# A start-up stretch on VectorE put in another order: the low parts of the first pair of batches

## The reference

```
q = rms_norm(layernorm(x) @ Wq)              # 32 heads of 128
k = rms_norm([context, layernorm(x)] @ Wk)   # 8 key heads, 256 keys per batch
v = [context, layernorm(x)] @ Wv
x = x + tanh(g) * (softmax(q k' / sqrt(128)) v) @ Wo
```

## Time and profile before

| | us |
|---|---|
| median of 3 runs | 1226.1 |
| lowest and highest | 1225.43, 1226.37 |
| the profiled execution | 1224.71 |
| its span in the trace | 1223.0 |
| TensorE busy | 1169.9 (96%) |
| VectorE busy | 832.4 (68%) |
| ScalarE busy | 588.2 (48%) |
| GpSimd busy | 348.8 (29%) |

### The profile page before, as it was taken

The page is one execution under the profiler, slowest core; times in us unless marked ns, Lnnn a source line. Parts: engine busy times, 40 slices in busy tenths (PEclk is TensorE's granted clock), DMA queues, the critical chain, the costliest instruction groups (busy, mean ns, idle before and its releaser), DMA issues.

```text
span 1223.0 us, 20618 instructions
## 1 busy us (share of the span) xinstructions
PE 1169.9 (96%) x6956; PEld 1005.2 (82%) x6956; DVE 832.4 (68%) x2373; ACT 588.2 (48%) x1364; POOL 348.8 (29%) x302
## 2 busy tenths in 40 slices
PE   7899999999999999999999999998999999899992
PEld 6798888988889888889888888887887777578871
DVE  6767667666676666676676776669788878784334
ACT  4545455454545545555454545445444455524441
POOL 5313022221312312132130321203343312445661
PEclk8999999999999999999999999999999999999996
DMA  7011000000101100010010000001212323833435
GB/s 275 1 36 52 2 35 18 35 34 0 51 0 34 31 20 34 0 51 0 34 51 0 34 0 1 1 1 54 83 55 74 106 69 103 321 126 126 144 103 206
DMA packets 37465, 73.57 MB, mean 60 GB/s; under 512 B 6098, under 2 KB 22482, under 8 KB 35366
## 3 DMA queue, kind: packets, MB, share of 16 engines
q1 hardware_dynamic: 30726, 56.38, 13.3%
q0 software_dynamic: 4960, 12.33, 3.2%
q10 hardware_dynamic: 1728, 4.20, 0.9%
HBM read 64.50 MB, written 12.32 MB: 63 GB/s over the span
## 4 chain that ended last, share of the span: by engine, by line
PE 59%; DVE 21%; issue 9%; ACT 5%; POOL 2%; DMA 2%; SPq 1%; DVEq 0%; ACTq 0%; POOLq 0%
PE bank L354 14%; PE bank L356 14%; PE bank L355 14%; PE bank L1978 5%; PE bank L1847 3%; DVE probs L1159 3%; ACT probs L790 3%; PE bank L1688 2%; PE bank L1989 2%; DVE k_junk L1116 2%; DVE iq L1322 2%; DVE row_max L1132 2%; DVE pt_lo L1146 2%; POOL k_rstd L577 1%; PE bank L1630 1%
## 5 line engine op out<-in xcount | busy, mean ns | idle before, releaser
L790 ACT ACTIVATE probs<-bank,exp_bias,q_rstd 128x256 f32<-128x256 f32 x256 | 141.3, 562 | 138.0 <-DVE exp_bias L1140 138.0
L1151 DVE TENSOR_TENSOR o_lo<-bank,o_hi 128x512 fp32r<-128x512 f32 x64 | 44.3, 692 | 178.6 <-ACT o_hi L783 178.6
L354 PE MATMUL bank<-wkv_hi,kv_src_lo 128*128 128x256 f32 x512 | 145.8, 285 | 1.4 <-DVE kv_src_lo L1184 1.4
L355 PE MATMUL bank<-wkv_lo,kv_src_hi 128*128 128x256 f32 x512 | 145.6, 284 | 0.0
L356 PE MATMUL bank<-wkv_hi,kv_src_hi 128*128 128x256 f32 x512 | 145.5, 284 | 0.0
L581 POOL TENSOR_TENSOR q_rstd<-q_var,minus_half 128x8 f32<-128x8 f32 x32 | 52.7, 1646 | 300.4 <-DVE q_var L1119 300.4
L779 ACT ACTIVATE pt_hi<-bank 128x512 fp32r<-128x512 f32 x128 | 69.6, 596 | 116.2 <-PE bank L1688 116.2
L354 PE MATMUL bank<-wo_hi,o_lo 128*128 128x512 f32 x256 | 104.2, 407 | 1.7 <-DVE o_lo L1151 1.2
L577 POOL TENSOR_TENSOR k_rstd<-k_var,minus_half 128x4 f32<-128x4 f32 x32 | 32.5, 1016 | 249.1 <-DVE k_var L1093 249.1
L354 PE MATMUL bank<-wq_hi,kv_src_lo 128*128 128x512 f32 x256 | 102.8, 401 | 0.8 <-POOL wq_lo L566 0.8
L356 PE MATMUL bank<-wo_hi,o_hi 128*128 128x512 f32 x256 | 101.5, 397 | 0.0
(11 more groups left out here) (257 smaller groups left out, 3090.6 us busy)
## 6 DMA issues: line engine op xcount, KB each, us to landing
weights<-r_w SPq DMA_DIRECT2D x16, 768.0 KB, 9.3
wq_raw<-wq SPq DMA_DIRECT2D x8, 1024.0 KB, 4.7
wo_raw<-wo SPq DMA_DIRECT2D x8, 1024.0 KB, 4.8
wkv_raw<-wkv SPq DMA_DIRECT2D x8, 512.0 KB, 3.3
gu_raw<-w_gate SPq DMA_DIRECT2D x10, 256.0 KB, 3.4
gu_raw<-w_up SPq DMA_DIRECT2D x10, 256.0 KB, 3.8
wd_raw<-w_down SPq DMA_DIRECT2D x10, 256.0 KB, 4.1
x_sb<-x SPq DMA_DIRECT2D x4, 512.0 KB, 9.8
```

What stands on the lines that cost most here:

```text
L354: eng.matmul(out_ap, a_lo, b_hi, start=start, stop=False)
L355: eng.matmul(out_ap, a_hi, b_lo, start=False, stop=False)
L790: act.activation(probs[:, h, :], scores_ps[h // 2][:, (h % 2) * 256:(h % 2) * 256 + 256], ACT.Exp, bias=exp_bias[:, h:h + 1], scale=q_rstd ...
L1151: dve.tensor_tensor(o_lo[:, par, :], o_ps[:, :], o_hi[:, par, :].bitcast(F32), ALU.subtract)\
```

## The change

On VectorE, `q_norm(0)` is cut in two. The sums of query tile 0 stay where they were. Then come the layer norm rows of the last pair, `k_low` and the first `q_low`, and only after them the sums of query tile 1 with `q_var`, then the second `q_low`. `low_pair(2)` goes behind that, and `low_pair(3)` moves out of the start into step 0 of the first group, between `bias_of` and `normalise`. On TensorE the wait of the first `kv_half` in the loop for six `kv_src_lo` tiles goes away. Nothing is computed that was not computed before, and no instruction is added.

```diff
-            def q_norm(pair):
-                for i in range(2):
+            def q_norm(pair, tiles=range(2)):
+                for i in tiles:
                     dve.wait_ge(q_copied, pair * 2 + (i + 1))
...
+                if tiles[-1] == 0:
+                    return
                 dve.wait_ge(q_ss_ready, pair * 8 + 8)
...
             stats_pair(3)
-            q_norm(0)
+            q_norm(0, range(0, 1))
             rows_pair(3)
             k_low(0, 0)
             q_low(0, 0, 0)
+            q_norm(0, range(1, 2))
+            q_low(0, 1, 0)
             low_pair(2)
-            q_low(0, 1, 0)
-            low_pair(3)
             dve.wait_ge(gates_ready, 1)
...
                     bias_of(n, b)
+                    if isinstance(g, int) and g == 0 and b == 0:
+                        low_pair(3)
                     if after_start(g, b, 1):
                         o_low(n - 1, (b - 1) % 2)
                     normalise(n)
...
                         if isinstance(g, int) and g == 0 and b < NB - 2:
                             pe.wait_ge(ctx_lo_ready, np_)
-                        if isinstance(g, int) and g == 0 and b == 0:
-                            pe.wait_ge(ln_lo_ready[0], 6)
                         (kv_half, q_half)[b % 2](ng, np_, 0)
```

## The result

| | before | after |
|---|---|---|
| median of 12 runs each, us | 1226.32 (1225.26 to 1232.04) | 1222.97 (1221.40 to 1225.82) |
| ratio | | 0.9969, 95% interval 0.9958 to 0.9981 |
| profiled execution, us (span) | 1224.71 (1223.0) | 1225.34 (1223.6) |

By the ratio the change makes the kernel 3.8 us faster, with 2.3 to 5.1 us as the interval; the two medians lie 3.35 us apart. 1223.2 us were predicted. The profiled execution of after is one of its slowest, and slower than that of before. Where it gained and where it lost is read stretch by stretch.

What follows compares the result with a forecast made beforehand. TensorE, busy for 96% of the span, was taken to bound the kernel, so only its start could shift. 2.77 + 0.27 - 0.1 = 2.9 us off 1226.1 gave 1223.2 us; 8-in-10 range 1222.4 to 1225.4.

Steps and rivals of the forecast that it cites:

- Step 1: VectorE behind tile 0's sums: layer norm rows come at once, 1.63 us earlier, and `k_lo` starts at 29.61.
- The first rival: VectorE: the idle 0.58 us stays where tile 0 ends; gain about 2.4 us, 1223.7; chance 0.18.
- Step 2: VectorE: `q_lo` at 30.27, tile 1's sums at 30.87, `q_var` at 31.84, which is 1.60 us later than before.
- Step 3: TensorE ahead of the transposes: idle time shrinks from 2.8 to 1.2 us, granted clock stays at 1.00.
- Step 4: GpSimd: `q_rstd` takes 1.64 us, first context instruction ends at 36.06, `exp_bias` on VectorE at 36.07, 2.77 us earlier.
- 3.0 us without a lock: VectorE: without the port lock `exp_bias` would be done at about 35.3; the gain would still be about 3.0 us.
- The third rival: VectorE: `exp_bias` does not get between the two context instructions and ends at 38.45; 1225.4; chance 0.10.
- Step 5: VectorE: `low_pair(3)` takes 1.2 us under the exponentials and costs nothing, with 1.1 us left.
- Step 6: VectorE and TensorE: second `v_lo` free at 40.05 after the projections; `k_norm` from 43.45 to 40.4, 3.0 us.
- Step 7: TensorE: with the wait kept, projections would start at 33.7 in place of 33.4; 0.3 us, not a term of its own.
- the 0.1 held back for the gap: Sum: 0.1 us subtracted because the idle 0.58 us ahead of VectorE's rows was taken as gone, though unknown.
- The clock rival: TensorE: not all runs before had the low clock, which costs about 1.1 us; gain only 1.8, 1224.3; chance 0.17.

Runs made afterwards that it cites:

- the 16 instructions: The kernel before with 16 one-element copies added on VectorE ahead of `stats_pair(2)`; ratio 0.9984 (0.9974 to 0.9995).
- the kernel with 24 transposes: The kernel before with 24 identity transposes added on TensorE ahead of its wait for `k_lo`; ratio 0.9997 (0.9983 to 1.0010).
- the long instruction: The changed kernel with GpSimd's `ctx_low(2)` and `ctx_low(3)` made one instruction of double width; ratio 0.9990 (0.9981 to 1.0000).
- the one behind `exp_bias`: The changed kernel with GpSimd waiting for `exp_bias` before its two context instructions; ratio 0.9989 (0.9976 to 1.0002).
- the two shifted kernels: The kernels before and after, each with the same 16 one-element copies added on VectorE; ratios to before 0.9984 and 0.9971.
- the pairs alone: The kernel before with only `low_pair(2)` and `low_pair(3)` moved and TensorE's wait removed, `q_norm` whole; ratio 1.0000 (0.9986 to 1.0014).
- the sums ahead of `q_low`: The changed kernel with query tile 1's sums ahead of the first `q_low` on VectorE; ratio 0.9979 (0.9969 to 0.9988).

## Why the prediction was right

The kernel became faster by the chain that was predicted, to 1222.97 us against 1223.2. That the two agree within 0.3 us is in part luck: the medians lie 3.35 us apart and the ratio gives 3.8, where 2.9 were forecast, and the median of before was 1226.1 in three runs and 1226.32 in twelve. In its own steps, with the 0.13 us in mind by which `ln_var` stands later in the profile of after:

- Step 1 (`k_lo` at 29.61 by taking the idle 0.58 as gone): 29.83. The gap is gone, as taken, and the rows cost 0.15 more than assumed: the second root ended at 29.33, not at 29.10, since it started 0.14 later and the two took 1.33 us beside the first row, not 1.24. The first rival, that the gap stays, fell: there is none in front of the rows, and 14.45 against 14.46 us says that none is left on the path. That it belongs to a place in VectorE's program is shown by the 16 instructions that remove it. What fills it is open. An instruction packet of 8 KB starts in the trace of before at 29.90, 1.21 us behind the gap's start, and at the same distance in both other profiles with the gap; with the 16 instructions it comes 1.9 us earlier behind `ln_var`. But the gap had ended at 29.27, so it was not a wait for this packet's data.
- Step 2 (`q_var` 1.60 later, at 31.84): 32.05, 1.81 later, from the 0.22 by which step 1 came later.
- Step 3 (idle time 1.2, clock 1.00): 1.30 and 1.00. The Trainium skill (TensorE: Matmul & The Clock Gate, "Part 1: The HAM clock gate") lets idle time close the gate; the rows on before (2.8 us idle, then 0.50) and the kernel with 24 transposes (0.21 us idle, 1.00) agree. The kernels with 2.42 us (1.00) and 1.91 us (0.50) show that more than the length of one idle time decides. In all eight kernels in which the idle time here was 1.19 to 1.32 us, the clock from 30 to 37 us was 1.00.
- Step 4 (`q_rstd` 1.64, first context end and `exp_bias` 36.07, 2.77 earlier): 1.65, 36.3 and 36.33, 2.51 earlier, or 2.64 without the shift of `ln_var`. The power took 1.65 in all eight kernels with `q_norm` cut and 1.88 or 1.89 in the four with it whole. That `exp_bias` gets in between two context instructions was the assumption of most weight. It holds: 36.33 with two, and 3.30 us for `exp_bias` with one long. The third rival (1225.4) falls with it, and the experiment that forces it costs 2.24 us. The Trainium skill (SBUF — State Buffer, "Who interferes with whom") has the lock as one for a whole instruction, and both kernels agree. The gain alone could not have shown it, since the prediction had 3.0 us without a lock too; the long instruction and the one behind `exp_bias` do.
- Step 5 (cover of `low_pair(3)` 1.1 us): 1.17 us of idle time are left.
- Step 6 (second `v_lo` tied with the projections, `k_norm` 40.4, 3.0 us): 40.67, 2.78 us. The 0.2 us between them are again step 1's. The tie is real: `v_lo` has no idle time in after, and 0.68 where `exp_bias` is earlier.
- Step 7 was mis-sized, without weight in the sum: the wait is worth 0.48 us, not 0.3, since the projections started 0.41 later behind `ln_var` and the first matmul took 0.36 us, not 0.28.

The sum was 2.9 us (2.77 + 0.27 - 0.1) and the stretch gives 2.91 (2.64 + 0.27): the 0.1 held back for the gap went to the second root. What it consists of was not in the prediction: 1.21 us are the clock, 0.45 the gap, and 1.25 what is left, the order by itself (1.26 between the two shifted kernels). The clock rival (1224.3) had the right price, 1.1 against 1.21. How many timed runs of before had the low clock can't be read, since they have no profile and only a mean clock of the whole run. Between 30 and 45 us it was there in the three profiles in which TensorE stood still for 2.8 us and more (before, the pairs alone, and the long context instruction at 41 us), and missing in the one with 2.42.

Open: the timed ratio gives 3.8 us, and the stretch 2.9. The interval holds both. The other kernels' ratios follow their gains in the stretch within their intervals, so I see no second cause, but none is excluded.

## What to carry to other kernels

A small instruction that another engine's long ones shut out costs what is left of the long one; here 0.16 us became 0.42 to 3.30. Bring it in front of a gap between two long ones, and check by the trace that it makes the gap, since 0.2 us decided over 2. Cutting a chain to feed the idle engine paid here only with the work moved out of the second chain's way; try each half alone before believing in either. And take the length of the changed stretch from each profile, beside timed runs: a span of one execution moved here by more than the effect, from a part that the change never reached.

## What the runs showed that I had not expected

- 16 instructions of 128x1 elements, added to a kernel that waits for VectorE, made it 2.0 us (0.6 to 3.2) faster. An idle 0.58 us left the critical chain, and in the profile, with TensorE's idle time down from 2.8 to 2.42 us, the granted clock stayed at 1.00.
- Of four `normalise` instructions beside GpSimd's context instruction only the first stood still, 2.40 us in place of 0.34; `exp_bias` loses 0.86 us in after (1.02 in place of 0.16).
- A granted clock of 0.50 right behind the changed stretch, with 1.91 us of idle time ahead of it, took 1.2 us from the kernel with the sums ahead of `q_low`; its 2.77 us of the stretch are not what it gained as a whole.
